# Down projection of a sparse feed-forward layer: the high part of the rows against both parts of the weights in one 512-column matmul

## The chip, the cores and the metric

The kernel runs on one core of a Trainium2 chip. Its time is the device time of one execution in microseconds (us), the median of three runs. The trace is one profiled execution of the same program. Engines are named as the profile names them: PE is TensorE (PEld its weight loads), DVE is VectorE, ACT is ScalarE, POOL is GpSimd and SP is SyncE. A name such as L1315 is a line of the kernel.

## The reference

The layer takes x (32 sequences of 256 rows of 256 values), a context of 77 rows for each sequence, and adds two terms to x. The second one is what this change touches:

```
x = x + tanh(g_xattn) * attention(layernorm(x), context)      # 16 heads
h = layernorm(x)                                              # 8192 rows of 256
gate = h @ gate_kernel                                        # 8 experts, the best 2 are kept
w = softmax over the two kept logits
for each kept expert e of a row:
    mid = silu(h @ w0[e]) * (h @ w1[e])                       # 256 -> 512
    x += tanh(g_ffn) * w * (mid @ wo[e])                      # 512 -> 256, the down projection
```

## The kernel before, in words

The program has two stages. In the first (about 750 us) it works through the attention, two tiles of 128 rows for each sequence. For each row it also writes two copies, one for each chosen expert, into a table in DRAM that is sorted by expert (`routed_rows`). Each copy carries the row's number and its weight. On the side, every weight of the experts is split into a high part (rounded to the matmul's reduced fp32 format, `fp32r`) and a low part (the rest), which go to DRAM and come back into one large tile, `w_all`, as the second stage starts.

The second stage is a loop over 135 tiles of 128 routed rows, `MOE_T`, one expert for each tile. Rows and weights are both held as a high and a low part, so a product is three products: high x high, high x low and low x high. That is what `PARTS` lists. In tile t the engines do the following.

- PE (`tile` in the tensor block) computes `up` of tile t with w0 (six matmuls of 512 columns into a bank of `banks4`, L1296), then `g_T` of tile t-1 (four transposes of the gated product into `psT`, L1304), `e_T` of tile t+1 (two transposes of the rows just loaded into `psG`, L1281), `up` with w1 (six more), and then `down` of tile t-1 (twelve matmuls of 256 columns into the first half of the bank `psB`, L1315). PE's loop is unrolled over eight tiles.
- ACT computes the silu (L721), copies the high part of the transposed product to `hgT` (`g_evac`, L727), the same for the next rows (`e_evac`, L715), and then in `y_evac` (L733) takes the down projection out of PSUM: one instruction that multiplies `psB` by the row's weight `ewt` and writes `ey`, which has two buffers. It waits for `ey_ps` (from `down`) and for `added`, which says that the buffer of two tiles ago has been sent.
- DVE computes the low parts (`g_low`, L1038, and `e_low`, L1043, with two small copies of the row's number and weight, L1047 and L1048) and the gated product (`glu`, L1034).
- POOL in its turn first runs `add_rows` of tile k: it waits for `ey_done`, and for the landing of the add before (`added`), and then issues an indirect DMA that adds the 128 rows of `ey` to the output in DRAM (L531). Behind it in the same queue it runs `load_rows` of tile k+4: it waits until tile k+2's rows have been used, and issues the load of 128 routed rows into `et` (L526), which has two buffers. `e_T` of tile k+4 waits for that load.

The order on each engine is the written order; there is no planner. Two semaphores go from `y_evac` onwards: `ey_done` lets POOL start `add_rows`, and lets PE start the next `down`, which writes `psB` again.

Of the kernel before, what the change touches and what calls it, by code (L numbers as in the profile page):

```python
# [10 lines left out]
ALU = mybir.AluOpType  # L11
ACT = mybir.ActivationFunctionType
# [9 lines left out]
def flamingo_gated_layer(nc, x, ctx_in, mask, g_xattn, g_ffn, Wq, bq, Wk, bk, Wv, bv, Wfc, bfc,  # L22
                         gate_kernel, w0, w1, wo, out):
    B, S, D = x.shape
# [4 lines left out]
    NT = B * QT  # L29
    DC = D // P  # L30
    E, _, F = w0.shape
    FC = F // P
    scale = float(HD) ** -0.5
# [22 lines left out]
    MOE_T = NT * TOP_K + E - 1  # L56
# [17 lines left out]
    with ExitStack() as ctx, ExitStack() as attention:  # L74
        memory = ctx

        def sb(name, shape, dt=F32):
            return memory.enter_context(nc.sbuf_tensor(name, shape, dt))

        def ps(name, shape, dt=F32):  # L80
            return ctx.enter_context(nc.psum_tensor(name, shape, dt))

        def sem(name):
            return ctx.enter_context(nc.semaphore(name))
# [7 lines left out]
        ey = sb("ey", [P, 2, D])  # L92
        eid = sb("eid", [P, 4], I32)
        ewt = sb("ewt", [P, 4])
        etT = sb("etT", [P, 2, 2, DC, P], F32R)
        hgT = sb("hgT", [P, 2, FC, P], F32R)
# [111 lines left out]
        w_all = sb("w_all", [P, NQ, 2, FR, F], F32R)  # L208
# [6 lines left out]
        psB = ps("psB", [P, 512])  # L215
# [30 lines left out]
        row_copy, row_id = sem("row_copy"), sem("row_id")  # L246
        passed = {e.engine: sem(f"passed{n}") for n, e in enumerate((nc.sync, nc.gpsimd, nc.vector))}

        tab, tab_done = sem("tab"), sem("tab_done")
        et_in, etT_ps, etT_hi, etT_lo, h0_ps, h1_ps = [sem("et_in0"), sem("et_in1")], sem("etT_ps"), sem("etT_hi"), sem("etT_lo"), sem("h0_ps"), sem("h1_ps")  # L250
        hs_done, hg_done, hgT_ps, hgT_hi, hgT_lo, ey_ps, ey_done, eid_done, added = (
            sem(n) for n in ("hs_done", "hg_done", "hgT_ps", "hgT_hi", "hgT_lo", "ey_ps", "ey_done", "eid_done", "added"))
# [17 lines left out]
        def tiles(eng, body, n=MOE_T, unroll=4):  # L270

            turns = n // unroll
            assert n - turns * unroll >= 2
            for u in range(unroll):
                body(u, u, 0)
            with eng.Fori(1, turns) as it:
                for u in range(unroll):
                    body(it * unroll + u, u, it)
            for u in range(n - turns * unroll):
                body(turns * unroll + u, u, turns)  # L280

        def known(v, least):

            return not isinstance(v, int) or v >= least

        def below(v, end):
            return not isinstance(v, int) or v < end
# [268 lines left out]
        def _(act):  # L556
# [172 lines left out]
            def y_evac(t, u):  # L729
                act.wait_ge(ey_ps, t + 1)  # L730
                if known(t, 2):
                    act.wait_ge(added, 16 * (t - 1))
                act.activation(ey[:, u % 2], psB[:, 0:D], ACT.Copy, scale=ewt[:, u:u + 1]).then_inc(ey_done, 1)  # L733

            e_evac(0, 0)

            def tile(t, u, q):
                silu(t, u)
                if known(t, 1):
                    g_evac(t - 1)  # L740
                if below(t, MOE_T - 1):
                    e_evac(t + 1, u + 1)
                if known(t, 1):
                    y_evac(t - 1, (u - 1) % 4)

            tiles(act, tile)
            g_evac(MOE_T - 1)
            y_evac(MOE_T - 1, (MOE_T - 1) % 4)


        @block.vector
        def _(dve):
# [252 lines left out]
            steps = [0]  # L1005
# [25 lines left out]
            def glu(t, u):  # L1031
                dve.wait_ge(h1_ps, t + 1)
                dve.wait_ge(hs_done, t + 1)
                dve.tensor_tensor(hs[:], banks4[:, 2 + u % 2], hs[:], ALU.mult).then_inc(hg_done, 1)  # L1034

            def g_low(t):
                dve.wait_ge(hgT_hi, t + 1)
                dve.tensor_tensor(hgT[:, 1].rearrange("p c q -> p (c q)"), psT[:], hgT[:, 0].rearrange("p c q -> p (c q)").bitcast(F32),  # L1038
                                  ALU.subtract).then_inc(hgT_lo, 1)

            def e_low(t, u):
                dve.wait_ge(etT_hi, t + 1)
                dve.tensor_tensor(etT[:, u % 2, 1].rearrange("p c q -> p (c q)"), psG[:, 0:D],  # L1043
                                  etT[:, u % 2, 0].rearrange("p c q -> p (c q)").bitcast(F32), ALU.subtract).then_inc(etT_lo, 1)
                if known(t, 4):
                    dve.wait_ge(added, 16 * (t - 3))
                dve.tensor_copy(eid[:, u:u + 1], et[:, u % 2, D:D + 1]).then_inc(eid_done, 1)  # L1047
                dve.tensor_copy(ewt[:, u:u + 1], et[:, u % 2, D + 1:D + 2]).then_inc(eid_done, 1)  # L1048

            e_low(0, 0)  # L1050

            def tile(t, u, q):
                if known(t, 1):
                    g_low(t - 1)
                if below(t, MOE_T - 1):
                    e_low(t + 1, (u + 1) % 4)
                glu(t, u)

            tiles(dve, tile)
            g_low(MOE_T - 1)  # L1060


        @block.tensor
        def _(pe):
            pe.wait_ge(ident_done, 2)
            pe.wait_ge(raw_in, 16 * 4)
            for n in range(4):
                for c in range(DC):
                    for o in range(DC):
                        m = pe.transpose(banks4[:, n, (c * DC + o) * P:(c * DC + o + 1) * P], raw[:, n, o, c * P:(c + 1) * P], ident[:])  # L1070
# [4 lines left out]
            PARTS = ((0, 0), (0, 1), (1, 0))  # L1075
# [210 lines left out]
            def weight(e, c, part, run, first=0, n=F):  # L1286

                at = ((c * 2 + part) * FR + run) * F + first
                return w_of[:, bass.ds(e, 1), at:at + n].rearrange("p o f -> p (o f)")

            def up(t, u, e, n, bank, done):
                steps = [(a, w, c) for a, w in PARTS for c in range(DC)]
                for j, (a, w, c) in enumerate(steps):
                    if n == 0 and (a, c) == (1, 0):
                        pe.wait_ge(etT_lo, t + 1)
                    m = pe.matmul(banks4[:, bank], etT[:, u % 2, a, c], weight(e, c, w, n), start=(j == 0), stop=(j == len(steps) - 1))  # L1296
                m.then_inc(done, 1)
# [9 lines left out]
            def down(t, e):  # L1307
                pe.wait_ge(hgT_hi, t + 1)
                if known(t, 1):
                    pe.wait_ge(ey_done, t)  # L1310
                steps = [(a, w, c) for a, w in PARTS for c in range(FC)]
                for j, (a, w, c) in enumerate(steps):
                    if (a, c) == (1, 0):
                        pe.wait_ge(hgT_lo, t + 1)
                    m = pe.matmul(psB[:, 0:D], hgT[:, a, c], weight(e, c // 2, w, 2, c % 2 * D, D), start=(j == 0), stop=(j == len(steps) - 1))  # L1315
                m.then_inc(ey_ps, 1)

            def expert_with_weights(t):
# [10 lines left out]
            def tile(t, u, q):  # L1329
                if u == 0:  # L1330
                    if known(t, 1):
                        expert[0], expert[-1] = (pe.snap(r, min_val=0, max_val=E - 1) for r in (next_expert, last_expert))
                    else:
                        expert[0] = expert_with_weights(t)
                pe.wait_ge(etT_hi, t + 1)
                if known(t, 2):
                    pe.wait_ge(hg_done, t - 1)
                up(t, u, expert[u], 0, u % 2, h0_ps)

                if below(t, MOE_T - 1):  # L1340
                    expert[u + 1] = expert_with_weights(t + 1)
                    if u == UNROLL - 1:
                        pe.reg_mov(next_expert, expert[u + 1])
                        pe.reg_mov(last_expert, expert[u])
                if known(t, 1):
                    g_T(t - 1)
                if below(t, MOE_T - 1):
                    e_T(t + 1, u + 1, (q * UNROLL + u + 1) // 2 if isinstance(q, int) else q * (UNROLL // 2) + (u + 1) // 2)
                up(t, u, expert[u], 1, 2 + u % 2, h1_ps)
                if known(t, 1):  # L1350
                    down(t - 1, expert[u - 1])

            UNROLL = 8
            tiles(pe, tile, unroll=UNROLL)
            g_T(MOE_T - 1)
            down(MOE_T - 1, expert[(MOE_T - 1) % UNROLL])


# [25 lines left out]
```

## Time and profile before

| what | value |
|---|---|
| median of 3 runs | 1440.11 us (1439.74 to 1444.11) |
| profiled execution, first to last instruction | 1441.3 us |
| PE busy | 1340.0 us, 93% of the span |
| PEld busy | 1173.3 us, 81% |
| POOL busy | 895.5 us, 62% |
| DVE busy | 808.2 us, 56% |
| ACT busy | 697.4 us, 48% |
| mean granted TensorE clock | 0.978 of full speed |
| data moved in DRAM | read 68.95 MB, written 70.27 MB |

Of the profiled execution only the span is given, and it stands 1.2 us above the median of the runs. Busy time is the time in which an engine had an instruction in work; idle time of an engine that sets no end costs nothing. In a timeline row the columns are: start in us, length in us, engine, line, operation, tiles written and read, count, and in brackets the idle time before it with what ended that.

### The profile page before, as it was taken

How to read it: one execution, taken by the hardware profiler on the slowest of the kernel's cores; microseconds unless marked ns; L12 is line 12 of the kernel's file. 1: busy time of each engine (PE TensorE's matmuls, PEld its weight loads, DVE VectorE, ACT ScalarE, POOL GpSimd, SP SyncE). 2: the span in 40 equal slices, each digit the busy share in tenths (PEclk: the TensorE clock that was granted, in tenths of full speed). 3: DMA queues.
4: the chain of work that ended last, by engine and by line, in shares of the span. 5: the costliest groups of instructions: out<-in, count | busy, mean ns of one | idle time of the engine just before them, and what ended most of it. 6: DMA issues, size and time to landing. Idle time of an engine off the chain costs nothing.

```text
span 1441.3 us, 35541 instructions
## 1 busy us (share of the span) xinstructions
PE 1340.0 (93%) x9634; PEld 1173.3 (81%) x9635; DVE 808.2 (56%) x2519; ACT 697.4 (48%) x1779; POOL 895.5 (62%) x1389
## 2 busy tenths in 40 slices
PE   3999999999999999999939999999999999999996
PEld 3898888888888888888827788888888888888885
DVE  3688788888788888888643333333333333333332
ACT  2566566566566566566513333333333333333332
POOL 3478888888888888888853344444444444444443
PEclk9999999999999999999959999999999999999998
DMA  5033313333313333313677784333333333333332
GB/s 148 18 112 120 119 58 108 123 118 115 117 61 108 123 118 115 117 61 108 205 209 211 200 220 80 54 51 55 54 51 58 52 51 54 55 51 52 58 52 38
DMA packets 73811, 139.70 MB, mean 97 GB/s; under 512 B 11568, under 2 KB 54992, under 8 KB 71600
## 3 DMA queue, kind: packets, MB, share of 16 engines
q0 software_dynamic: 32064, 52.46, 18.5%
q1 hardware_dynamic: 39696, 84.87, 18.2%
q10 hardware_dynamic: 2016, 1.93, 0.5%
q8 instruction: 19, 0.31, 0.1%
q14 instruction: 16, 0.13, 0.0%
HBM read 68.95 MB, written 70.27 MB: 97 GB/s over the span
## 4 chain that ended last, share of the span: by engine, by line
PE 53%; issue 13%; POOL 11%; DVE 10%; DMA 6%; ACT 5%; POOLq 1%; DVEq 1%; ACTq 0%; SPq 0%; another core or an unknown queue 0%
PE banks L1296 23%; PE psB L1315 12%; PE banks L1137 4%; PE psT L1304 3%; DMA out_dram<-ey,eid 3%; POOL routed_rows L478 2%; DMA et<-routed_rows 2%; PE psG L1281 2%; ACT prob L604 2%; PE psT L1149 2%; PE banks L1089 2%; ACT prob L608 2%; DVE qT L809 2%; PE psB L1161 1%; POOL rs L421 1%
## 5 line engine op out<-in xcount | busy, mean ns | idle before, releaser
L531 POOL DMA_INDIRECT out_dram<-ey,eid x135 | 217.3, 1609 | 374.8 <-issue 141.0
L1296 PE MATMUL banks<-w_all,etT 128*128 x1620 | 434.2, 403 | 0.7 <-ACT etT L715 0.7
L1038 DVE TENSOR_TENSOR hgT<-psT,hgT 128x512 fp32r<-128x512 f32 x135 | 93.4, 692 | 430.4 <-ACT hgT L727 430.4
L1296 PEld LDWEIGHTS banks<-w_all,etT 128*128 128x128 f32 x1620 | 287.0, 190 | 51.4 <-issue 3.4
L1315 PEld LDWEIGHTS psB<-w_all,hgT 128*128 128x128 f32 x1620 | 208.1, 188 | 17.9 <-issue 1.3
L1315 PE MATMUL psB<-w_all,hgT 128*128 x1620 | 216.9, 283 | 0.8 <-ACT hgT L727 0.8
L733 ACT ACTIVATE ey<-psB,ewt 128x256 f32<-128x256 f32 x135 | 64.1, 475 | 240.4 <-DMA out_dram<-ey,eid 180.1
L721 ACT ACTIVATE hs<-banks 128x512 f32<-128x512 f32 x135 | 80.7, 598 | 186.1 <-PE psT L1304 181.5
L432 POOL TENSOR_TENSOR kbd<-kT,own 128x616 fp32r<-128x616 f32 x128 | 152.4, 1222 | 24.3 <-DVE kT L831 24.3
L1161 PE MATMUL psB<-vbd,probT 128*128 128x51 f32 x1280 | 160.0, 273 | 0.0
L1161 PEld LDWEIGHTS psB<-vbd,probT 128*128 128x128 f32 x1280 | 157.2, 194 | 1.6
L478 POOL DMA_INDIRECT routed_rows<-rows,slot x128 | 130.3, 1018 | 42.5 <-issue 23.0
L599 ACT COPY probT<-psT 128x512 f32<-128x512 f32 (+1 forms) x192 | 100.9, 526 | 101.5 <-PE psT L1149 98.6
L1137 PE MATMUL banks<-kbd,qT 128*128 128x308 f32 (+2 forms) x768 | 136.3, 327 | 0.0
L526 POOL DMA_DIRECT2D et<-routed_rows x135 | 126.8, 939 | 13.7 <-issue 13.7
L1149 PE MATMUL psT<-ident,prob 128*128 128x128 f32 x640 | 106.4, 281 | 25.4 <-ACT prob L608 19.9
L1137 PEld LDWEIGHTS banks<-kbd,qT 128*128 128x128 f32 x768 | 117.3, 193 | 11.4 <-issue 0.5
L860 DVE TENSOR_REDUCE mx<-banks 128x12 f32<-128x924 f32 (+1 forms) x128 | 100.9, 792 | 32.9 <-PE banks L1137 20.1
L1149 PEld LDWEIGHTS psT<-ident,prob 128*128 128x128 f32 x640 | 73.4, 150 | 46.2 <-issue 37.4
L1034 DVE TENSOR_TENSOR hs<-banks,hs 128x512 f32<-128x512 f32 x135 | 92.1, 682 | 3.9 <-PE banks L1296 3.5
L1304 PEld LDWEIGHTS psT<-ident,hs 128*128 128x128 f32 x540 | 67.3, 141 | 17.8 <-issue 0.2
L1304 PE MATMUL psT<-ident,hs 128*128 128x128 f32 x540 | 80.9, 272 | 0.0
(159 smaller groups left out, 2309.3 us busy)
## 6 DMA issues: line engine op xcount, KB each, us to landing
split_weights<-w_part SPq DMA_DIRECT2D x16, 1536.0 KB
w_all<-split_weights SPq DMA_DIRECT2D x32, 768.0 KB
et<-routed_rows POOLq DMA_DIRECT2D x135, 129.0 KB, 3.3
xb<-in_x_dram SPq DMA_DIRECT2D x32, 256.0 KB, 2.8
w_raw<-in_L_ffn_w_kernel_dram SPq DMA_DIRECT2D x32, 256.0 KB
out_dram<-x SPq DMA_DIRECT2D x64, 128.0 KB
w_raw<-in_L_ffn_wo_kernel_dram SPq DMA_DIRECT2D x16, 256.0 KB
cb<-in_ctx_dram SPq DMA_DIRECT2D x32, 77.0 KB
```

What stands on the lines that cost most here:

```text
L432: gp.tensor_tensor(kbd[:, u, a, c], kT2[:, a, c].bitcast(F32).rearrange("p (o k) -> p o k", o=1).to_broadcast([P, HC, K2]), own[:].rearran ...
L478: gp.indirect_dma_start(out=routed, out_offset=bass.IndirectOffsetOnAxis(ap=slot[:, u4, k:k + 1], axis=0), in_=rows[:, u4, k, :], in_offse ...
L526: gp.dma_start(et[:, u % 2], routed[bass.ds(r * P, P), :]).then_inc(et_in[u % 2], 16)
L531: gp.indirect_dma_start(out=out, out_offset=bass.IndirectOffsetOnAxis(ap=eid[:, u:u + 1], axis=0), in_=ey[:, u % 2, :], in_offset=None, co ...
L599: act.copy(probT[:, c0:c1].rearrange("p c q -> p (c q)"), psT[:, 0:(c1 - c0) * P]).then_inc(t_sb, 1)
L860: dve.tensor_reduce(mx[:, t, h0:h0 + n * k].rearrange("p (n h) -> p n h", n=n), sv, AX_X, ALU.max).then_inc(s_max, 1)
L1137: m = pe.matmul(psS[:, n, (h0 - first) * K2:(h1 - first) * K2], qT[:, u, q_part, c, t * P:(t + 1) * P], kbd[:, u, k_part, c, h0 - c * HC:h ...
L1149: m = pe.transpose(psT[:, (c - c0) * P:(c - c0 + 1) * P], prob[:, t, c * P:(c + 1) * P], ident[:])
L1161: m = pe.matmul(psB[:, h * VW:(h + 3) * VW], probT[:, c], vbd[:, u, c].rearrange("p h d -> p (h d)"), start=(c == 0), stop=(c == CH - 1), ...
L1296: m = pe.matmul(banks4[:, bank], etT[:, u % 2, a, c], weight(e, c, w, n), start=(j == 0), stop=(j == len(steps) - 1))
L1304: m = pe.transpose(psT[:, c * P:(c + 1) * P], hs[:, c * P:(c + 1) * P], ident[:])
L1315: m = pe.matmul(psB[:, 0:D], hgT[:, a, c], weight(e, c // 2, w, 2, c % 2 * D, D), start=(j == 0), stop=(j == len(steps) - 1))
```

## The change

In `down` the four matmuls of the high rows with the high weights and the four of the high rows with the low weights become four matmuls of 512 columns. Their moving operand, `weight_pair`, takes 256 columns of the high part and the 256 columns of the low part that belong to them, 1536 elements further on in `w_all`. The high x high sum lands in `psB[:, 0:256]`, the high x low sum in `psB[:, 256:512]`. Then the four matmuls of the low rows with the high weights add to the first half. `y_evac` on ACT now takes the second half, scaled, into `ey`, and signals the new semaphore `ey_low`. A new DVE function, `y_sum`, waits for that, computes `psB[:, 0:256] * ewt + ey` in place, and signals `ey_done`. In DVE's order `y_sum` of tile t-1 stands behind `glu` of tile t.

```diff
@@ ACT, y_evac
-                act.activation(ey[:, u % 2], psB[:, 0:D], ACT.Copy, scale=ewt[:, u:u + 1]).then_inc(ey_done, 1)
+                act.activation(ey[:, u % 2], psB[:, D:2 * D], ACT.Copy, scale=ewt[:, u:u + 1]).then_inc(ey_low, 1)
@@ DVE
+            def y_sum(t, u):
+
+                dve.wait_ge(ey_low, t + 1)
+                dve.scalar_tensor_tensor(out=ey[:, u % 2], in0=psB[:, 0:D], scalar=ewt[:, u:u + 1], in1=ey[:, u % 2], op0=ALU.mult, op1=ALU.add).then_inc(ey_done, 1)
+
@@ DVE, tile
                 glu(t, u)
+                if known(t, 1):
+                    y_sum(t - 1, (u - 1) % 4)
 
             tiles(dve, tile)
             g_low(MOE_T - 1)
+            y_sum(MOE_T - 1, (MOE_T - 1) % 4)
@@ PE
+            wo_of = w_all[:].rearrange("p (e c) s r f -> p e c s r f", c=DC)
+
+            def weight_pair(e, c):
+                return wo_of[:, bass.ds(e, 1), c // 2, :, 2, c % 2 * D:(c % 2 + 1) * D].rearrange("p o s d -> p (o s) d")
+
@@ PE, down
-                steps = [(a, w, c) for a, w in PARTS for c in range(FC)]
-                for j, (a, w, c) in enumerate(steps):
-                    if (a, c) == (1, 0):
-                        pe.wait_ge(hgT_lo, t + 1)
-                    m = pe.matmul(psB[:, 0:D], hgT[:, a, c], weight(e, c // 2, w, 2, c % 2 * D, D), start=(j == 0), stop=(j == len(steps) - 1))
+                for c in range(FC):
+                    pe.matmul(psB[:, 0:2 * D], hgT[:, 0, c], weight_pair(e, c), start=(c == 0), stop=False, skip_group_check=True)
+                pe.wait_ge(hgT_lo, t + 1)
+                for c in range(FC):
+                    m = pe.matmul(psB[:, 0:D], hgT[:, 1, c], weight(e, c // 2, 0, 2, c % 2 * D, D), start=False, stop=(c == FC - 1), skip_group_check=True)
                 m.then_inc(ey_ps, 1)
```

## Rows read from the trace of the kernel before

**Rows 1.** The page's first section: busy us, share, instructions.
```profile
PE 1340.0 (93%) x9634; PEld 1173.3 (81%) x9635; DVE 808.2 (56%) x2519; ACT 697.4 (48%) x1779; POOL 895.5 (62%) x1389
```
**Rows 2.** Busy time by stretch: length, PE, PEld, DVE, ACT, POOL, clock, DMA share, GB/s.
```profile
753.00:925.00 172.00, 164.67 (x974) 141.16 (x975) 58.22 (x167) 61.04 (x131) 69.91 (x64) 0.98 0.65 159
925.00:1430.00 505.00, 503.18 (x3078) 438.03 (x3077) 178.38 (x509) 187.08 (x409) 226.42 (x203) 1.00 0.33 53
```
**Rows 3.** Groups from 925 to 1430 us: busy us, mean ns, idle before, releasers.
```profile
L1296 PE MATMUL banks<-w_all,etT 128*128 x1224 | 326.2, 402 | 0.0
...
L1315 PE MATMUL psB<-w_all,hgT 128*128 x1240 | 166.3, 283 | 0.8 <-ACT hgT L727 0.8
...
L1315 PEld LDWEIGHTS psB<-w_all,hgT 128*128 128x128 f32 x1239 | 159.0, 188 | 14.2 <-issue 1.3
...
L733 ACT ACTIVATE ey<-psB,ewt 128x256 f32<-128x256 f32 x103 | 48.9, 475 | 179.2 <-DMA out_dram<-ey,eid 149.1 <-PE psB L1315 30.1
```
**Rows 4.** The chain of waits from 1100 us on: start, length, what, matmuls.
```profile
1105.34 1.43 PE psB L1315 x12
1106.77 1.40 PE banks L1296 x6
1108.16 0.44 PE psT L1304 x4
1108.60 0.22 PE psG L1281 x2
```
**Rows 5.** The timeline of two tiles from 1180 to 1192 us.
```profile
1181.25 0.47 ACT L733 ACTIVATE ey<-psB,ewt 128x256 f32<-128x256 f32 x1 [1.71 <-DMA out_dram<-ey,eid]
...
1182.74 1.61 POOL L531 DMA_INDIRECT out_dram<-ey,eid  x1 [2.64 <-issue]
...
1183.54 0.58 ACT L727 CAST hgT<-psT 128x512 fp32r<-128x512 f32 x1
1183.98 0.99 POOL L526 DMA_DIRECT2D et<-routed_rows  x1
...
1184.15 0.69 DVE L1038 TENSOR_TENSOR hgT<-psT,hgT 128x512 fp32r<-128x512 f32 x1 [3.11 <-ACT hgT L727]
...
1187.66 0.38 PE L1281 MATMUL psG<-ident,et 128*128 128x128 f32 x2
...
1190.98 0.47 ACT L733 ACTIVATE ey<-psB,ewt 128x256 f32<-128x256 f32 x1 [1.71 <-DMA out_dram<-ey,eid]
```
**Rows 6.** The tile `et`, the load of rows, from 925 to 1430 us.
```profile
DMA to landing us min/median/max: 2.3/3.3/3.4
```
**Rows 7.** The chain of waits from 1136 to 1152 us.
```profile
1143.68 0.31 POOL out_dram L531
...
1144.92 3.42 DMA et<-routed_rows
1148.34 0.04 issue
```
**Rows 8.** Who waited, from 753 to 925 us: us in total, times, longest.
```profile
PE psG L1281 <- DMA et<-routed_rows: 21.9, 8, 15.3
```
**Rows 9.** The chain of waits from 765 to 800 us.
```profile
785.04 4.51 DMA et<-routed_rows
...
793.25 0.48 ACT ey L733
```
**Rows 10.** DVE's groups by shape, whole span.
```profile
L1043 DVE TENSOR_TENSOR etT<-psG,etT 128x256 fp32r<-128x256 f32 x135 | 56.1, 415 | 11.3 <-ACT etT L715 11.2
L888 DVE SCALAR_TENSOR_TENSOR x<-banks,tanhg,xg 128x256 f32<-128x256 f32 x64 | 30.7, 480 | 17.8 <-PE banks L1177 17.8
```
**Rows 11.** The tile `ey`, the add of rows, from 925 to 1430 us.
```profile
DMA to landing us min/median/max: 3.7/3.9/4.0
```
**Rows 12.** A late start: POOL's timeline from 1036 to 1046 us.
```profile
1042.32 0.57 POOL L526 DMA_DIRECT2D et<-routed_rows  x1 [1.04 <-issue]
```
**Rows 13.** Who waited, from 925 to 1430 us: us in total, times, longest.
```profile
PE psG L1281 <- DMA et<-routed_rows: 1.1, 2, 0.6
```

More of the change, by code:

```diff
@@ L247, in flamingo_gated_layer @@
         passed = {e.engine: sem(f"passed{n}") for n, e in enumerate((nc.sync, nc.gpsimd, nc.vector))}
-        tab, tab_done = sem("tab"), sem("tab_done")
+        tab, tab_done, ey_low = sem("tab"), sem("tab_done"), sem("ey_low")
         et_in, etT_ps, etT_hi, etT_lo, h0_ps, h1_ps = [sem("et_in0"), sem("et_in1")], sem("etT_ps"), sem("etT_hi"), sem("etT_lo"), sem("h0_ps"), sem("h1_ps")
```

## The prediction, made before the changed kernel was run

> **What bounds the kernel now.** I read the page's busy shares first, then the stretches, then the groups by line, the chain of waits, and last the timeline of single tiles. The page says PE 93% [rows 1], and the stretches say where that comes from. From 925 us to 1430 us PE is busy for 503.18 of 505.00 us at the full granted clock (1.00), while DVE, ACT and POOL have 178 to 226 us of work [rows 2]. The group of L733 has 103 instructions there [rows 3], one for each tile, so a tile takes 505 / 103 = 4.90 us. The chain of waits gives the tile's parts as steps of PE alone: up 1.40 us, g_T 0.44, e_T 0.22, down 1.43 [rows 4], and up again 1.40, together 4.89. So PE's order of instructions bounds the steady tiles, and none of it waits (0.8 us in 1240 matmuls of L1315 [rows 3]).
>
> A second thing is nearly as long, and a busy share can't show it. It is a loop through POOL over two tiles. When y_evac of tile k is done, POOL adds tile k (L531) and behind it issues the load for tile k+4 (L526); e_T of k+4 waits for that load, up and down follow, and y_evac of k+2 closes the loop. From the timeline [rows 5]: y_evac ends at 1181.25 + 0.47 = 1181.72. L531 starts at 1182.74, 1.02 later. L526 starts at 1183.98, 1.24 later. Its rows land 3.3 us after that in the median [rows 6]. After a landing PE needs 0.04 to start [rows 7]. From the transposes at 1187.66 to the end of the y_evac after next, 1190.98 + 0.47, it is 3.79 us. Sum: 1.02 + 1.24 + 3.3 + 0.04 + 3.79 = 9.39 us for two tiles. PE takes 9.80 for two. The loop has 0.41 us to spare for each pair of tiles, 0.2 us for each.
>
> Twice the trace shows this loop in charge. From 753 to 925 us, while the weights still come in (159 GB/s), e_T waits for its rows 8 times [rows 8, 2]; the chain there runs L733, L526, 4.51 us of DMA, PE, L733 [rows 9]. And at 1148 us a late add makes a late load, and the chain goes through the load for 3.42 us [rows 7].
>
> **The change part by part.**
>
> *PE.* Removed: eight matmuls of 256 columns in each tile. Added: four of 512. Four of 256 stay. Down takes 1.43 / 12 = 0.119 us for a matmul of 256 columns, up takes 1.40 / 6 = 0.233 for one of 512 [rows 4]. New down: 4 x 0.233 + 4 x 0.119 = 1.41 us, 0.02 less. Times 135 tiles that is 2.7 us. The columns that stream through are as many as before (12 x 256 = 4 x 512 + 4 x 256), which is why so little goes. The operand in two pieces of 256 columns has no row. Its bounds: two times the 256-column matmul, 0.238, with which nothing is saved (1.43), and from the other side, a price by matmuls and not by columns, 8 x 0.119 = 0.95 us, which saves 0.48. I take 0.233, since the matmul of up is the same shape in and out. The weight loads fall from twelve to eight, 0.188 us each [rows 3]; they lie beside matmuls, as the twelve, 2.26 us in sum, fit into a down of 1.43.
>
> The Trainium skill (TensorE: Matmul & The Clock Gate, section Back-to-back issue gap) says that the spacing of matmuls in a stream is set by the weight load and the matmul together, and gives 131 ns for 512 columns; by that four 512-column matmuls would take 0.52 us. No row here agrees: six of 512 columns take 1.40 us, 0.233 each.
>
> The wait for the low part of the rows (`hgT_lo`) comes after four matmuls of 0.233 where it came after eight of 0.119, 0.93 against 0.95 us, with g_low issued at the same moment. Nothing changes.
>
> *ACT.* y_evac has the same shape, other columns, the same waits: 0.475 us as before [rows 3], cost nothing.
>
> *DVE.* Added: `y_sum`, 135 instructions. The same operation in the same shape (scalar_tensor_tensor, 128 x 256, one input from PSUM) is L888, 0.480 us [rows 10]. A hand-over from ACT to DVE is short: L727 ends at 1183.54 + 0.58 = 1184.12, L1038 starts at 1184.15 [rows 5]. So `ey_done` comes 0.03 + 0.48 = 0.51 us later. Bounds: 0.45 with the cheaper L1043 (0.415) [rows 10], 0.72 with L1038 (0.69, twice the columns) [rows 5]. In DVE's queue `g_low` of the next tile stands behind `y_sum`, and before it DVE idles 3.11 us [rows 5]; y_sum lies in that idle time, so as work it costs nothing. PE's next down waits for `ey_done` too, but g_low, which precedes that down, comes only after DVE's idle time; that wait stays hidden.
>
> *POOL.* Its instructions are the same, but all of them, add and load, start 0.51 us later after down, because `add_rows` stands in the queue ahead of `load_rows`. Here is the price. The loop becomes 9.39 + 0.51 - 0.02 = 9.88 us, 4.94 for a tile. PE alone would need 4.90 - 0.02 = 4.88. The loop takes over. The add's own chain (each add waits for the landing of the one before) is 3.9 us [rows 11] and some 0.9 to 1.0 to the next L531, at most 4.9; it is shifted as a whole and stays just under the new period. The end of the loop over eight tiles on PE lies between down and up, outside the loop through POOL, and is absorbed by PE's new idle time.
>
> *Sum.* Against the profiled execution:
> - steady tiles, about 118 (from the middle of the first stretch on): 4.94 - 4.90 = 0.04 each, 4.4 us;
> - late starts: in five places from 925 us on a load starts 0.8 to 1.4 us late, as at 1042.32 [rows 12] and before 1148 [rows 7]. Up to now 0.41 us of that was free, now it is not: 5 x 0.4 = 2 us;
> - the tiles that already wait: 7 of the 8 waits of [rows 8] (the first is the stage's start), each one round of the loop, longer by 0.51 - 0.02: 3.4 us;
> - the last tile, where nothing lies beside y_sum: 0.5 us.
>
> Together +10.3 us: a span of 1451.6. That execution stands 1.2 us above the median, so the median comes to 1450.4; I say 1450. The likeliest case alone reaches from 1445 to 1460, by the bounds of y_sum and the spread of the landings (2.3 to 3.4 us).
>
> **The rivals.**
>
> *A. The slack holds it (0.24).* The loop's sum rests on medians; with landings nearer to 3.1 us, or a start of L531 0.1 us earlier, the loop has 0.6 to spare and 0.51 is swallowed. For it speaks that of the hundred loads after 925 us only two were waited for [rows 13]; against it that the early stretch waits already. What is left is PE's gain and the end: -2.7 + 0.5, with the early tiles +2: the median within 1437 to 1443, no change.
>
> *B. The matmul costs by the piece (0.05).* Then down loses 0.48 us, PE needs 4.42, and the loop 9.39 + 0.51 - 0.48 = 9.42, 4.71 a tile: 0.19 less for 118 tiles, 22 us, 1418. Only the bound above speaks for it, [rows 4] speak against. The rule of the skill named above would have this sign, since the loop would then be the bound in the same way.
>
> *C. y_sum is dearer than its shape (0.07).* If reading `psB` right behind ACT, or writing `ey` in place, or the signal from DVE to POOL costs another 0.5 us, the loop is 10.4, 5.2 a tile: 0.3 x 118 = 35 us more, 1480. It decides from a total delay of 1.0 us. Against it: L1038 starts 0.03 us after ACT on the same bank `psT`.
>
> *D. The split operand is slow (0.04).* Each 512-column matmul that reads two pieces would have to take 0.3 us instead of 0.233: down 0.27 longer, loop 10.17, 5.08 a tile, 0.18 x 118 = 21 us, with the rest 1467.
>
> **How the numbers follow.** Forecast 0.60, A 0.24, B 0.05, C 0.07, D 0.04. A measurement of this kernel can tell about 0.3% from no change, 4.3 us. Faster by more than that: B, and a small part of A, 0.07. Within it: most of A and the lower edge of the forecast, 0.25. Slower: the rest, 0.68. The range reaches down to A's lower end and up over the forecast's own range, 1437 to 1463; B, C and D lie outside.
>
> **What would show it.** Right: in the changed trace PE has idle time before L1281 in most steady tiles, ended by the DMA of `et`; the down groups last 1.41 us; y_sum takes 0.48 us and starts 0.03 us after y_evac; L531 starts 1.0 us after y_sum; a tile takes 4.94 us; POOL's and ACT's means are unchanged. Wrong: if PE is still busy for more than 99% of the steady stretch (A), if down lasts less than 1.2 us (B), if y_sum or its hand-over is over 0.8 us (C), or if the spacing of the wide matmuls is over 0.25 us (D).

## The result, and the profile after

The changed kernel takes 1460.34 us in the median of 6 runs (1454.0 to 1465.1), the kernel before 1443.72 us over the 6 runs beside it. The ratio is 1.010, with a 95% interval of 1.0075 to 1.0125: 1.0% slower. (The quotient of the two medians would be 1.0115; this document gives the recorded ratios throughout.) The prediction said 1450 us (1437 to 1463), slower, through the load of rows. The direction, the place and the steady price were right. The gain on PE was put too small. The profiled executions also lose more in the early tiles than forecast, but how much of that the delay causes stays open.

Of the executions of the kernel before that ran beside the experiments, one was slow (2007.56 us at a granted clock of 0.613) and is in no ratio.

The profiled execution has a span of 1460.2 us, 18.9 more than before. The busy shares of the page hardly move:

```profile
PE 1344.5 (92%) x9094; PEld 1146.5 (79%) x9095; DVE 873.2 (60%) x2654; ACT 699.0 (48%) x1779; POOL 895.3 (61%) x1389
```

540 matmuls and 540 weight loads are gone (9634 to 9094), 135 DVE instructions came, and still PE's busy time is 4.5 us larger than in [rows 1]: this number shows neither the gain nor the loss. The stretches that answer to [rows 2]:

```profile
753.00:925.00 172.00, 156.28 (x783) 127.69 (x782) 67.72 (x181) 56.71 (x121) 63.47 (x59) 0.95 0.61 155
925.00:1430.00 505.00, 501.32 (x2642) 413.00 (x2641) 226.77 (x611) 186.07 (x408) 225.92 (x204) 1.00 0.32 53
```

In the early stretch PE's busy time falls from 164.67 to 156.28 us and the mean granted clock from 0.98 to 0.95. In the steady one PE is idle for 3.68 us against 1.82, so it still counts as busy for 99.3%. The groups there, in the columns of [rows 3]:

```profile
L1325 PE MATMUL psB<-w_all,hgT 128*128 x408 | 110.0, 391 | 0.0
...
L1328 PE MATMUL psB<-w_all,hgT 128*128 x408 | 64.8, 281 | 0.0
...
L1053 DVE SCALAR_TENSOR_TENSOR ey<-psB,ewt,ey 128x256 f32<-128x256 f32 x101 | 48.9, 484 | 81.8 <-ACT ey L733 81.8
L733 ACT ACTIVATE ey<-psB,ewt 128x256 f32<-128x256 f32 x102 | 48.6, 476 | 184.0 <-PE psB L1328 181.6 <-DMA out_dram<-ey,eid 2.4
L1289 PE MATMUL psG<-ident,et 128*128 128x128 f32 x202 | 42.6, 293 | 3.7 <-DMA et<-routed_rows 3.2
...
L1289 PEld LDWEIGHTS psG<-ident,et 128*128 128x128 f32 x202 | 21.3, 141 | 15.9 <-DMA et<-routed_rows 12.4
```

y_sum (L1053) takes 0.484 us, y_evac is as it was, and the two transposes of e_T (L1289) now wait for their rows. The wait stands mostly at PEld. Who waited in that stretch, to be held against [rows 13]:

```profile
PEld psG L1289 <- DMA et<-routed_rows: 12.4, 41, 1.2
PE psG L1289 <- DMA et<-routed_rows: 3.2, 8, 0.9
```

The chain of waits shows the same delay as longer steps of PE. These are three tiles in a row, to be held against the 0.22 us of L1281 in [rows 4]:

```profile
1118.14 0.37 PE psG L1289 x2
...
1123.11 0.27 PE psG L1289 x2
...
1127.97 0.34 PE psG L1289 x2
```

So PE's busy share hides most of the loss. From the first transpose of g_T to the next `up` it is 0.573 us in the median before the change and 0.692 after it; 64 of 101 steady tiles are more than 0.05 us above 0.573, and together they are 14.5 us above it. Only 3.68 us of idle time are written down at PE.

One round of the loop in the timeline, with the same columns as [rows 5]:

```profile
1181.45 0.48 ACT L733 ACTIVATE ey<-psB,ewt 128x256 f32<-128x256 f32 x1 [1.84 <-PE psB L1328]
1181.96 0.48 DVE L1053 SCALAR_TENSOR_TENSOR ey<-psB,ewt,ey 128x256 f32<-128x256 f32 x1 [0.84 <-ACT ey L733]
...
1183.38 1.61 POOL L531 DMA_INDIRECT out_dram<-ey,eid  x1 [2.70 <-DVE ey L1053]
...
1184.37 0.69 DVE L1038 TENSOR_TENSOR hgT<-psT,hgT 128x512 fp32r<-128x512 f32 x1 [1.92 <-ACT hgT L727]
...
1184.63 0.96 POOL L526 DMA_DIRECT2D et<-routed_rows  x1
...
1188.03 0.20 PEld L1289 LDWEIGHTS psG<-ident,et 128*128 128x128 f32 x2 [0.26 <-DMA et<-routed_rows]
...
1191.38 0.48 ACT L733 ACTIVATE ey<-psB,ewt 128x256 f32<-128x256 f32 x1 [1.92 <-PE psB L1328]
1191.89 0.48 DVE L1053 SCALAR_TENSOR_TENSOR ey<-psB,ewt,ey 128x256 f32<-128x256 f32 x1 [0.93 <-ACT ey L733]
```

The reader can walk it. y_evac ends at 1181.93, y_sum starts 0.03 later and ends at 1182.44. L531 follows 0.94 us later, L526 another 1.25 later. The weight loads of the transposes, with PEld idle before them and released by the DMA, start at 1188.03, 3.40 after L526, and the second y_sum ends at 1192.37. From the end of the one y_sum to the end of the other it is 9.93 us for two tiles, and this round has no slack. L1038 is still preceded by 1.92 us of DVE's idle time, so y_sum as work costs DVE nothing.

**Where the time went.** From the starts of L733 one can count tiles. The table gives the stretches of the profiled executions; "again" is a second execution of the same program.

| | first y_evac | per tile, tiles 0 to 32 | per tile, tiles 32 to 134 | from the last y_evac to the end | span |
|---|---|---|---|---|---|
| before | 765.2 | 5.163 | 4.900 | 11.1 | 1441.3 |
| before, again | 770.3 | 5.232 | 4.895 | 10.9 | 1447.9 |
| changed | 764.3 | 5.573 | 4.949 | 12.7 | 1460.2 |
| changed, again | 767.3 | 5.428 | 4.950 | 12.9 | 1458.8 |

The first pair differs by 13.1 us in the 32 early intervals, 5.0 us in the 102 steady ones, 1.6 at the end and -0.9 ahead of the stage: 18.8 of 18.9. The steady number repeats to 0.005 us; the early one scatters. Over both pairs the early loss is (5.50 - 5.20) x 32 = 9.7 us, 13.1 in the first and 6.3 in the second. Of the 1.6 us at the end 0.5 are y_sum of the last tile; the rest wasn't followed up.

### The profile page after: what moved, and what is told of

It is laid out like the page before. It is cut to its first block, busy times and chain, and to the rows that moved or that the text cites. A ratio compares the mean times of both kernels' runs of the same rounds, so it can differ in the third digit from the quotient of the medians.

```text
span 1460.2 us, 34056 instructions
## 1 busy us (share of the span) xinstructions
PE 1344.5 (92%) x9094; PEld 1146.5 (79%) x9095; DVE 873.2 (60%) x2654; ACT 699.0 (48%) x1779; POOL 895.3 (61%) x1389
## 4 chain that ended last, share of the span: by engine, by line
PE 47%; issue 14%; POOL 11%; DVE 11%; DMA 9%; ACT 5%; POOLq 1%; DVEq 1%; ACTq 0%; SPq 0%; another core or an unknown queue 0%
PE banks L1309 19%; PE psB L1325 7%; DMA et<-routed_rows 5%; PE banks L1145 4%; PE psB L1328 4%; PE psT L1317 3%; PE psG L1289 3%; DMA out_dram<-ey,eid 3%; POOL routed_rows L478 3%; ACT prob L604 2%; PE psT L1157 2%; PE banks L1097 2%; ACT prob L608 2%; DVE qT L809 2%; POOL rs L421 1%
## 5 line engine op out<-in xcount | busy, mean ns | idle before, releaser
L531 POOL DMA_INDIRECT out_dram<-ey,eid x135 | 217.2, 1609 | 394.3 <-DVE ey L1053 125.3
L1038 DVE TENSOR_TENSOR hgT<-psT,hgT 128x512 fp32r<-128x512 f32 x135 | 93.4, 692 | 258.8 <-ACT hgT L727 256.7
L733 ACT ACTIVATE ey<-psB,ewt 128x256 f32<-128x256 f32 x135 | 64.3, 476 | 252.5 <-PE psB L1328 243.5
L1325 PE MATMUL psB<-w_all,hgT 128*128 x540 | 148.3, 397 | 0.8 <-ACT hgT L727 0.8
L526 POOL DMA_DIRECT2D et<-routed_rows x135 | 126.6, 938 | 14.1 <-issue 14.1
L1053 DVE SCALAR_TENSOR_TENSOR ey<-psB,ewt,ey 128x256 f32<-128x256 f32 x135 | 65.3, 484 | 116.8 <-ACT ey L733 116.8
L1325 PEld LDWEIGHTS psB<-w_all,hgT 128*128 128x128 f32 x540 | 101.1, 191 | 26.4 <-issue 1.6
L1328 PEld LDWEIGHTS psB<-w_all,hgT 128*128 128x128 f32 x540 | 84.0, 192 | 11.3
```

The costliest lines, as they stand in the source:

```text
L526: gp.dma_start(et[:, u % 2], routed[bass.ds(r * P, P), :]).then_inc(et_in[u % 2], 16)
L531: gp.indirect_dma_start(out=out, out_offset=bass.IndirectOffsetOnAxis(ap=eid[:, u:u + 1], axis=0), in_=ey[:, u % 2, :], in_offset=None, co ...
L1325: pe.matmul(psB[:, 0:2 * D], hgT[:, 0, c], weight_pair(e, c), start=(c == 0), stop=False, skip_group_check=True)
L1328: m = pe.matmul(psB[:, 0:D], hgT[:, 1, c], weight(e, c // 2, 0, 2, c % 2 * D, D), start=False, stop=(c == FC - 1), skip_group_check=True)
```

## The experiments

Theory: y_sum delays `ey_done`; POOL's queue passes the delay on to the load behind the add, and e_T waits for the load. Rivals: the wide matmuls with their operand in two pieces cost; DVE's instruction, the shared bank or the hand-over cost by themselves; the chain of adds is the next bound.

**The wide matmuls alone.**

```diff
-                act.activation(ey[:, u % 2], psB[:, D:2 * D], ...).then_inc(ey_low, 1)
+                act.activation(ey[:, u % 2], psB[:, 0:D], ...).then_inc(ey_done, 1)
-                    y_sum(t - 1, (u - 1) % 4)
```

> The wide matmuls alone: down as in the changed kernel, but ACT's y_evac takes psB[:, 0:256] and signals ey_done itself, and there is no y_sum (the high x low part of the down projection is left out of the output). Theory (the sum delays ey_done, and through POOL's queue the load of rows): nothing is late any more, PE bounds again. Down 1.41 us, a steady tile 4.88 us, e_T not waiting after the first 33 tiles; time = before - 3 us, and the changed kernel's loss is gone. Rival (reading two pieces of weights 6 KB apart is what costs): the loss stays, before + 10 us or more.

Measured: 0.9947 of before (0.9926 to 0.9967), so 0.5% faster, some 7.7 us where 3 were expected. A steady tile takes 4.830 us, and the waits for rows are as few as before:

```profile
PEld psG L1281 <- DMA et<-routed_rows: 1.7, 3, 0.7
PE psG L1281 <- DMA et<-routed_rows: 0.9, 2, 0.5
```

In the steady tiles the split operand costs nothing, and the matmuls bring more than predicted. The steady loss lies in the other half of the change. The early tiles are less clear. They took 5.381 us each in this trace, against 5.163 and 5.232 before, though nothing delays `ey_done` here, and PEld waited for rows almost as long as in the changed kernel (753 to 925 us):

```profile
PEld psG L1281 <- DMA et<-routed_rows: 16.3, 11, 2.5
```

The profiled execution was 4 us slower than this kernel's median (1443.96 against 1439.81), and the median leaves no room for a loss in the early tiles: it is 7.7 us below before, and the steady tiles give 6.9 of that. So a single trace of that stretch can be some 5 us off by scatter alone.

**The sum alone.**

```diff
-                for c in range(FC):
-                    pe.matmul(psB[:, 0:2 * D], hgT[:, 0, c], weight_pair(e, c), ...)
...
+                steps = [(a, w, c) for a, w in PARTS for c in range(FC)]
+                for j, (a, w, c) in enumerate(steps):
...
+                    m = pe.matmul(psB[:, w * D:(w + 1) * D], hgT[:, a, c], weight(e, c // 2, w, 2, c % 2 * D, D), ...)
```

> The sum alone: twelve matmuls of 256 columns as before, but the four of the low weights write psB[:, 256:512]; ACT and DVE as in the changed kernel. Same output. Theory: the loss is all here: down 1.43 us, the loop through the load 0.02 us longer than in the changed kernel, 4.96 us a steady tile, the first 33 tiles as slow as in the changed kernel (5.5 us each); time = the changed kernel + 0 to 3 us, before + 13 to 18. Rival (the wide matmuls cost): before + 0 to 3 us.

Measured: 1.0108 of before (1.0063 to 1.0153), 5.004 us a steady tile against an expected 4.96, and 5.67 an early one. The loss appears without a wide matmul in the program, which settles it against the first rival. Of the 0.055 us by which a steady tile is above the changed kernel's, the 0.04 us that down is longer give 0.02 in a loop over two tiles; the rest wasn't followed up.

**The load ahead of the add in POOL's queue, in both kernels.**

```diff
-                if known(t, 2):
-                    add_rows(t - 2, (u - 2) % 4)
                 if below(t, MOE_T - 2):
                     load_rows(t + 2, u + 2)
+                if known(t, 2):
+                    add_rows(t - 2, (u - 2) % 4)
```

> The changed kernel with the two calls in POOL's tile swapped: load_rows of tile t+2 is issued before add_rows of tile t-2, so that the load no longer waits for ey_done. Theory: the loop through POOL is open; the load starts about 2 us earlier against PE, e_T waits nowhere in the steady stretch, a tile takes 4.88 us, the first 33 tiles come down to about 5.0 us each, and the time falls below the kernel before: before - 3 to - 8 us. Rival 1 (DVE's extra instruction or the shared bank slow PE or ACT by themselves): a steady tile stays at 4.94 us or more, before + 5 to + 15. Rival 2 (the add's own chain, 4.8 to 4.9 us a tile, is the next bound): the tile at 4.88 to 4.92 us with ACT's y_evac or POOL waiting for landings of the add, time within 3 us of before.

> The kernel before with the same swap in POOL's tile. Theory: the steady tiles were bound by PE, so nothing changes there (4.90 us); only the waits for rows in the first 33 tiles go, 5.16 us each down to about 5.0: before - 4 to - 7 us. It should stand 2 to 3 us above the changed kernel with the swap, the difference of the matmuls. Rival (adds behind loads come later, and their chain takes over): before + 0 or more.

Measured: the changed kernel with the swap 0.9846 of before (0.9809 to 0.9883), 22 us faster; the kernel before with the swap 0.9895 (0.9859 to 0.9930), 15 us faster. Both gains are larger than expected (3 to 8 and 4 to 7 us below before). Tiles take 4.865 us early and 4.813 steady in the first, 4.948 and 4.887 in the second. In the changed kernel the two stretches account for most of the gain: against the mean of the two traces of before, 10.7 us early and 8.6 steady. In the kernel before they account for some 9 of the 15 us; the rest lies outside them and wasn't followed up. The timeline of the changed kernel with the swap:

```profile
1181.83 0.48 DVE L1053 SCALAR_TENSOR_TENSOR ey<-psB,ewt,ey 128x256 f32<-128x256 f32 x1 [0.69 <-ACT ey L733]
1182.08 0.57 POOL L526 DMA_DIRECT2D et<-routed_rows  x1 [2.06 <-issue]
...
1182.89 0.38 PE L1289 MATMUL psG<-ident,et 128*128 128x128 f32 x2
```

The load now starts while y_sum is still at work, 0.25 us after y_sum's start and not 2.67 us as above, and no idle time stands before L1289. PE's stretches there are full:

```profile
753.00:925.00 172.00, 170.38 (x901) 142.02 (x902) 78.16 (x210) 64.16 (x139) 73.52 (x68) 0.98 0.66 162
925.00:1400.00 475.00, 475.00 (x2557) 397.70 (x2556) 218.40 (x589) 179.51 (x393) 214.01 (x197) 1.00 0.35 55
```

The same y_sum, bank and hand-over are in this kernel, and it is the fastest of those shown so far. So none of them costs anything by itself that a steady tile of 4.81 us would show, and the chain of adds isn't the bound at 4.81 us a tile. The kernel before had the same loop in charge in its early tiles, which is why the swap helps it too. The swap does a second thing: L526 takes 0.57 us in it and not 0.94, as the last section tells, so the size of its gain isn't the price of the queue order alone.

**The dose.** y_sum over half the columns, and y_sum done twice.

```diff
@@ half
-                dve.scalar_tensor_tensor(out=ey[:, u % 2], in0=psB[:, 0:D], ..., in1=ey[:, u % 2], ...)
+                dve.scalar_tensor_tensor(out=ey[:, u % 2, 0:D // 2], in0=psB[:, 0:D // 2], ..., in1=ey[:, u % 2, 0:D // 2], ...)
@@ twice
+                dve.scalar_tensor_tensor(out=psA[:, 0:D], in0=psB[:, 0:D], ..., in1=ey[:, u % 2], ...)
                 dve.scalar_tensor_tensor(out=ey[:, u % 2], in0=psB[:, 0:D], ..., in1=ey[:, u % 2], ...)
```

> The changed kernel with y_sum over 128 of the 256 columns (the high x high part of the other half is left out of the output). Theory (loop through the load over two tiles, 9.89 us in the changed kernel): y_sum takes about 0.34 us, the loop is 9.75, 4.87 us a tile against PE's own 4.83: 4.88 a steady tile, between the wide matmuls alone (4.83) and the changed kernel (4.95), and the time about the same as before (before - 3 to + 6 us). Rival (a cost of any DVE access to the bank or of the extra hand-over, whatever its length): as the changed kernel, before + 12 to + 17.

> The changed kernel with the sum done twice in a row on DVE, the first time into an idle PSUM bank: ey_done another 0.48 us later, output as before. Theory: the loop is 9.89 + 0.48 = 10.37 us, 5.19 us a steady tile, 0.24 more for each of 102 tiles, 24 us, and some 5 to 10 us more in the first 33 tiles: the changed kernel + 28 to 35 us, before + 43 to 52. Rival (the add's own chain or PE is the bound): the changed kernel + 0 to 5 us.

> The same doubled sum, with load_rows ahead of add_rows in POOL's queue. Theory: ey_done may be 1.0 us later and costs nothing, since only the add waits for it: steady tile 4.81 to 4.83 us as with the plain sum and this order, total within 2 us of that kernel, before - 19 to - 24 us. Rival (DVE's time or the hand-over counts by itself, or the add's chain becomes the bound): 5 us or more above the plain sum with this order.

Measured, with the wide matmuls alone and the changed kernel as the points between:

| y_sum | us from y_evac's start to `ey_done` | steady tile | ratio to before |
|---|---|---|---|
| none | 0.47 | 4.830 | 0.9947 |
| half | 0.86 | 4.902 | 1.0023 (0.9994 to 1.0052) |
| whole | 0.99 | 4.949 | 1.0100 (1.0075 to 1.0125) |
| twice | 1.38 | 5.153 | 1.0224 (1.0180 to 1.0268) |
| twice, load ahead | 1.38 | 4.816 | 0.9830 (0.9793 to 0.9868) |

```profile
L1053 DVE SCALAR_TENSOR_TENSOR psA<-psB,ewt,ey 128x256 f32<-128x256 f32 x91 | 44.8, 492 | 90.1 <-ACT ey L733 90.1
L1054 DVE SCALAR_TENSOR_TENSOR ey<-psB,ewt,ey 128x256 f32<-128x256 f32 x91 | 43.1, 474 | 0.0
```

From the whole to twice, 0.39 us more delay costs 0.204 us a tile, a half of it: that is what a loop over two tiles does. From half to whole, 0.13 us more costs 0.047. From none to half, 0.39 us cost only 0.072: by the theory PE's own time is the bound for the first part of the delay. The expectation for "half" held (+3.3 us, in -3 to +6), though its steady tile was 4.902 and not 4.88. The one for "twice" was too high: its median and its profiled execution are both 26 us above the changed kernel's, its ratio only 0.0124 (18 us), against 28 to 35 expected. The second sum added 0.39 us and not 0.48, since the two overlap; the 24 us for the steady part were 21, and the early tiles grew by 4, not by 5 to 10. With the load ahead, `ey_done` may come 0.91 us later than without a y_sum, and a steady tile stays at 4.82 us or less.

**The early and the late tiles apart.** The swap for the first 36 tiles only, and from tile 36 on only, with the changed kernel again beside them.

```diff
@@ swap early (in swap late, True and False change places)
+                if load_first and below(t, MOE_T - 2):
+                    load_rows(t + 2, u + 2)
                 if known(t, 2):
                     add_rows(t - 2, (u - 2) % 4)
-                if below(t, MOE_T - 2):
+                if not load_first and below(t, MOE_T - 2):
                     load_rows(t + 2, u + 2)
...
+            with gp.Fori(1, 9) as it:
+                for u in range(4):
+                    tile(it * 4 + u, u, True)
+            with gp.Fori(9, MOE_T // 4) as it:
+                for u in range(4):
+                    tile(it * 4 + u, u, False)
...
```

> The changed kernel with the load ahead of the add in POOL's queue for the first 36 tiles only (the stretch in which the weights still come in); from tile 36 on the order as it was. Theory (the changed kernel loses about 5 us in the steady stretch and 8 to 13 in the early one): the first 33 tiles at 4.9 us each as in the run with the swap throughout, the steady tiles at 4.95: before - 3 to - 7 us. Rival (the early excess of the profiled execution was chance, its median is near the 3.4 us of the prediction): this stands less than 8 us below the changed kernel.

> The same the other way round: the order as it was for the first 36 tiles, the load ahead of the add from tile 36 on. Theory: steady tiles at 4.82 to 4.83 us, 0.12 less for 99 tiles, 12 us below the changed kernel; the early stretch keeps its 5.4 to 5.6 us a tile: before + 0 to + 5 us. Rival as above: before - 5 us or less.

> The changed kernel again, beside the two above on the same chip. Every theory: before + 12 to 18 us. How its first 33 tiles differ from the 5.57 us each of the first trace shows how far that stretch scatters; if the half-clock windows (three there between 793 and 824 us) are a consequence of PE's waits for rows, there are some again in that stretch.

> The kernel before again, for its trace alone. If the early stretch scatters by chance, its first 33 tiles may take up to 5.4 us each as in the run of the wide matmuls alone, with a half-clock window; if not, 5.16 us each again and none.

Measured beside the same runs of before: changed again 1.0073 (1.0054 to 1.0092), swap early 0.9927 (0.9900 to 0.9954), swap late 0.9987 (0.9960 to 1.0014). The early swap takes away 1.46%, 21 us, and the late one 0.86%, 12.5 us. Together from 1.0073 they give 0.9841, and the swap throughout had 0.9846: the two stretches add up. The steady part came out near its forecast (12 us), so that the late swap stands 1.9 us below before, where 0 to 5 above were expected. The early one brought more: 10.6 us below before, where 3 to 7 were expected. In the traces the early tiles go to 4.884 us in the one, the steady ones to 4.818 in the other, and the untouched stretch stays (4.947 and 5.507). The 21 us of the early swap are more than the change lost there, since before the change there were already waits for rows in that stretch, and the swap removes those too. The kernel before, again, had 5.232 us an early tile and one stretch at the lower clock: by the expectation's own measure that stretch does scatter.

The early stretch from 760 to 925 us in four of them: before, before again, changed, changed with the early swap.

```profile
760.00:925.00 165.00, 158.36 (x959) 136.51 (x958) 57.13 (x161) 58.53 (x127) 69.35 (x63) 1.00 0.65 159
```
```profile
760.00:925.00 165.00, 157.86 (x928) 135.64 (x929) 54.56 (x157) 57.65 (x124) 66.20 (x61) 0.98 0.65 163
```
```profile
760.00:925.00 165.00, 149.94 (x765) 122.85 (x764) 66.12 (x175) 54.19 (x117) 62.52 (x58) 0.97 0.61 155
```
```profile
760.00:925.00 165.00, 163.92 (x873) 136.44 (x872) 75.13 (x201) 60.74 (x134) 71.57 (x66) 0.99 0.68 166
```

PE is idle for about 7 us there before the change, 15 after it (12 in the second execution), 1 with the swap. PEclk there shows a second effect. Between 785 and 925 us the granted clock stands at the lower of its two levels (1.2 GHz of 2.4) for 3.4 us at a time: never and once in the two executions before, three times and twice in the two after, twice with the late swap only, once with the wide matmuls alone, and never in the kernels in which the load goes ahead in the early tiles. In those of before, again, both of changed, wide matmuls alone and late swap each fall came at the end of a wait of PE for rows of 1.9 to 2.8 us, or at most 1.4 us after it; not every such wait was followed by one (2.9 us at 803 us with the late swap). No run held PE's waits and changed the clock alone. In the changed kernel, from 792.04 us on, a round of up, wide matmuls and narrow ones took 1.83, 1.71 and 0.85 us with the lower clock in it, where 1.40, 0.91 and 0.47 are usual: 1.6 us for one time. That is an estimate of some 3 of the 9.7 us, for two times more in the mean.

## Why the prediction was right, and where it was off

**What bounds, and the loop.** The mechanism was right. The loop was put at 9.88 us, 4.94 a tile; the trace has 9.90 (2 x 4.949). y_sum was priced at 0.48 from a row of the same shape and took 0.484; the hand-over of 0.03 is 0.03; POOL's two starts are where they were, 0.94 and 1.25 us in the round shown. The swap and the dose show that the delay reaches PE through the queue order: with the load behind the add each 0.39 us of delay costs 0.204 us a tile, with the load ahead 0.91 us cost nothing.

Two of the prediction's own signs were badly set. It would have called itself wrong (A) if PE stayed busy for more than 99% of the steady stretch, and PE did, with 501.32 of 505.00 us. And it wanted idle time before L1281 in most tiles; the profile has it in 41 of 101 at PEld and in 8 at PE itself. Yet the loss is there, and it is one of waiting for rows: it shows as the longer time around L1289, in 64 of 101 tiles. A share of busy time couldn't decide this, since PE's records go on through most of the wait.

**The step on PE failed in its size.** "0.02 less" a tile and "2.7 us" in sum: the two kernels with the load ahead show the difference undisturbed, 4.887 against 4.813 us, 0.074 a tile, ten us in 135. Two parts of it were missed. Down alone fell from 1.438 us (median) to 1.394, as the matmuls of 512 columns are 0.230 apart and the narrow ones kept 0.119. And once in eight tiles, where PE's loop turns, the kernel before took about 0.25 us more from down to the end of the next up. These rows of the kernel before show it: down starts at 1194.12 and up 1.60 us later, up then takes 1.48; one tile later the two are 1.46 and 1.40, so 0.22 less.

```profile
1194.12 1.61 PE L1315 MATMUL psB<-w_all,hgT 128*128 x12
1195.72 1.64 PE L1296 MATMUL banks<-w_all,etT 128*128 x6
1197.20 0.60 PE L1304 MATMUL psT<-ident,hs 128*128 128x128 f32 x4
...
1199.25 1.63 PE L1315 MATMUL psB<-w_all,hgT 128*128 x12
1200.71 1.55 PE L1296 MATMUL banks<-w_all,etT 128*128 x6
1202.11 0.60 PE L1304 MATMUL psT<-ident,hs 128*128 128x128 f32 x4
```

Of 96 downs from 925 to 1400 us 11 were so long, every eighth one; in the kernels with the wide matmuls none of 96 to 98, and six of 94 in the kernel with the sum alone. Down has four matmuls and four weight loads fewer with the wide matmuls; that this hides the turn is argued and not shown, and what the turn waits for stays open. In the changed kernel this gain was invisible, since the loop through POOL set the pace; so this error did not move the forecast of the time much.

**The early tiles** may be another mis-sized term. "7 of the 8 waits", 3.4 us, counted the rounds that waited already. With the delay others began to wait: 16 or 17 waits of PEld from 760 to 925 us instead of 9 or 10, 16 to 19 us instead of 9. The traces put the loss at 9.7 us over two pairs, of which the clock may be 3. But the wide matmuls alone show 11 waits and 16.3 us without any delay, so part of this is scatter between executions. From the times of all executions, an estimate: 14.4 and 10.6 us in total, less 5.0 to 5.6 for the steady tiles and 1.6 to 2.0 at the end, leaves 7.8 and 3.0 us for the rest, the early tiles above all, against 3.4 forecast. How much the term was off stays open. That further rounds begin to wait is what the doubled sum supports, with 17 waits and 23.7 us at PEld from 753 to 925 us. The slack of rounds that don't wait yet has to be counted in the crowded stretch too, not only in the steady one.

**Late starts and the steady sum.** 4.4 + 2 us were forecast for the steady tiles, and 5.0 and 5.6 measured in the two pairs. The 2 us for late starts weren't measured apart. The end took 1.6 and 2.0 us more, not 0.5.

**The rivals.** A (the slack holds it) fell with the steady tile: 4.949 us, and 4.902 with half of y_sum, against 4.830 without one. The ratio of 1.0023 for half isn't slack either, but the delay's cost against the gain on PE. B and D fell with the wide matmuls alone (down 1.398 us, the wide ones 0.231 apart), C with the row of L1053 and its hand-over (0.03 + 0.484 us). The sum came to +10.3, the timing says +14.4 (10.8 to 18.0) and, in the later session, +10.6 (7.8 to 13.3) on 1450 us. The forecast of 1450 stood on a median of 1440.11; the six executions of before that the changed kernel is held against have a median 3.6 us higher, which is a part of the 10 us between 1450 and 1460.34 and no error of the sum.

The Trainium skill (SBUF — State Buffer, section Who interferes with whom) says that a DVE instruction with at most one input from SBUF, outside the modes that use two ports, doesn't contend with GpSimd. y_sum reads the tensor `psB` from PSUM and the tensor `ey` from SBUF. In the changed kernel with the swap it lies beside L526 in 97 of 99 rounds (as at 1181.83 and 1182.08) and takes 0.483 us in the median, against 0.484 in the changed kernel, where it never does; L526 takes 0.572 us there and 0.570 in the kernel before with the swap, which has no y_sum: the traces agree.

## What to carry to other kernels

An instruction that fits into an engine's idle time can still cost time, when it stands between a result and the queue that passes it on: ask what is issued behind the consumer in the same queue, and how much slack that has. Two requests in one queue that wait for different things should stand in the order in which their conditions come true; here the swap of two calls was worth 1% in the kernel before; with it the change is worth another 0.5% (0.9895 to 0.9846), without it the change costs 1%. And once a loop over two tiles is the bound, each delay in it costs half its length a tile (0.39 us: 0.204), so its price can be estimated before anything is built. Whether such a loop is in charge can't be read from a busy share: here it stayed at 99.3%.

## What the hardware showed that was not expected

- The turn of PE's loop shows as about 0.25 us once in eight tiles with twelve matmuls in down, and not at all with eight.
- L526, the issue of the load of rows on POOL, takes 0.57 us when it starts outside the add's 1.6 us, and 0.96 on average when it starts inside them (3 and 97 times from 925 to 1430 us before the change). With the swap it never starts inside them in the kernel before and takes 0.569 us on average, so the swap shortens it as well.
- The granted clock fell to its lower level for 3.4 us two or three times in the changed kernel's early tiles, each time at the end of a wait of PE for rows of 1.9 to 2.8 us or shortly after it.
